# Attention B's score units issued in pairs, with three probability buffers and most other products through PSUM bank 7

## The chip, the cores and the metric

The kernel runs on one core of one Trainium2 chip. The metric is the device time of one execution in microseconds (us). A core has five engines that run side by side: TensorE (PE in the profile; PEld is its weight loads), VectorE (DVE), ScalarE (ACT), GpSimd (POOL) and SyncE (SP, which here issues all DMAs). They are ordered only by semaphores.

## What is computed

A block of four residual layers on x of 16 batches x 512 tokens x 128 channels, all float32:

```python
x = x + attn_a(layernorm(x))   # 16 heads of 64; softmax of q over d, of k over tokens; context = q^T k, then v
x = x + ffn(layernorm(x))      # xr, xk = mix of x and x one token before; sigmoid(xr Wr) * (relu(xk Wk)^2 Wv)
x = x + attn_b(layernorm(x))   # 16 heads of 8, rotary embedding:
#   scores = einsum('bhqd,bhkd->bhqk', q, k) / sqrt(8); attn = softmax(scores); ctx = attn @ v; ctx @ W_O
x = x + ffn(layernorm(x))
```

Attention B has 16 x 16 x 512 x 512 scores, and each goes through an exponential: this and the exponentials of attention A's q and k are ScalarE's main work.

## The kernel before

**Software pipeline.** The program is a row of 20 iterations, i = 0 to 19 (FUSED = NB + 4), written out for each engine by hand. In iteration i the engines work on five batches at once: a = i (attention A: projections, exponentials, context), s = i-1 (the end of attention A and the first feed-forward layer, f1), l = i-2 (layer norm and projections for attention B), b = i-3 (attention B's scores) and e = i-4 (the end of attention B and the second feed-forward layer, f2). Iterations 0 to 2 fill the pipeline (`filling_step`), 4 to 15 have all five stages, 16 to 19 drain it.

**Units.** An iteration has 16 units, n = 0 to 15. In each, TensorE issues `proj_half(n)` (three 512-column products into bank 4: a quarter of a token chunk's q and k), `scores(n)` (four products of 32 rows x 128 columns at four row positions of the array, into banks 0 to 3: four heads, 128 keys, 512 queries), and `weigh_values(n-1)` (four products with 32-column tiles at four column positions, into bank 6: probabilities times values). ScalarE answers with `exp_half(n)` (bank 4, 512 columns) and `exp_scores(n)` (banks 0 to 3, 2,048 columns) into one of two probability buffers. `scores(n)` waits until `exp_scores(n-1)` has emptied the banks, `proj_half(n+1)` until `exp_half(n)` has emptied bank 4.

**The rest** of a batch stands at fixed units between these (the table `places`): `context` (four calls a batch, 16 products each, of 64-column tiles), `ctx_wout`, `wv_ctx_wout`, `attn_out`, `heads_out`, `proj_b` (three parts), four groups of four transposes, and `ffn_k`, `ffn_r`, `ffn_v` for each feed-forward layer. Float32 products run as two passes (eight matmuls for four products). The k and r products and the transposes of h1 go through bank 4, and so lie in line with the projections; the others go through banks 5 and 7. VectorE or ScalarE copies each result out, and the order on each engine is the order in the code.

**Names.** `hold(engine, signal, batch, count)` is a wait. `s_exp`, `s_mm`, `ph_exp`, `ph_mm` count finished score and projection exponentials and products; `pv` counts weighed units; `p_ev` copies of `proj_b`; `h1_sb` the copy of h1's transpose; `t_ev`, `m_ev` the copies of `ctx_wout` and `wv_ctx_wout`.

## Time and profile before

| | |
|---|---|
| median of three runs | 1050.62 us (1045.62, 1050.62, 1050.64) |
| the profiled execution | 1045.19 us, span of its instructions 1043.4 us |
| TensorE matmul busy | 951.9 us (91%) |
| ScalarE busy | 735.1 us (70%) |
| VectorE busy | 610.4 us (58%) |
| GpSimd busy | 507.7 us (49%) |
| granted TensorE clock, mean | 0.971 |
| start of the score products of i = 3, 4, 10, 11, 16, 17 | 105.16, 168.77, 519.55, 577.98, 869.27, 929.15 us |

The starts of successive iterations can be read in the timeline from the first score products of each (four matmuls, L1493, or L1510 where the scores are split). A busy TensorE is not a TensorE at its peak: its matmuls overlap, and the time from one start to the next says more than a duration.

### The profile page before, as it was taken

What the parts mean: (1) busy time and instruction counts of PE and PEld (TensorE: products, weight loads), DVE (VectorE), ACT (ScalarE), POOL (GpSimd) and SP (SyncE); (2) the same over time, 40 slices, a digit from 0 to 9 for tenths busy, and PEclk for the clock granted to TensorE, in tenths of its full rate; (3) what the DMA queues carried; (4) which work ended last, traced back from release to release, by engine and by line L of the source; (5) the groups of instructions that cost most, each with busy time, mean ns of one, the idle gap of its engine ahead of it and who ended that gap; (6) DMA issues with size and microseconds to landing.
All of it is one profiled execution on the core that took longest, in us unless ns stands there. A gap on an engine that the chain in (4) does not pass through costs nothing.

```text
span 1043.4 us, 21070 instructions
## 1 busy us (share of the span) xinstructions
PE 951.9 (91%) x8139; PEld 510.9 (49%) x8139; DVE 610.4 (58%) x1475; ACT 735.1 (70%) x772; POOL 507.7 (49%) x344
## 2 busy tenths in 40 slices
PE   5985889999999999999999999999999999597983
PEld 3874534545454555545454545545554544232322
DVE  5776446566573847556573847656574745655233
ACT  4554667877777777878777777878777776375860
POOL 3758163644727292744637382754637271425000
PEclk9999889999999999999999999999999999798995
DMA  6002222324132332324132232324132232223210
GB/s 174 8 31 90 68 97 69 125 58 133 46 107 87 88 97 83 120 72 127 48 113 78 83 97 82 117 71 132 46 110 69 72 111 72 81 66 101 74 34 15
DMA packets 68657, 87.44 MB, mean 84 GB/s; under 512 B 13633, under 2 KB 40130, under 8 KB 68546
## 3 DMA queue, kind: packets, MB, share of 16 engines
q1 hardware_dynamic: 68546, 85.96, 27.4%
q8 instruction: 69, 1.13, 0.5%
q14 instruction: 42, 0.34, 0.1%
HBM read 16.19 MB, written 20.97 MB: 36 GB/s over the span
## 4 chain that ended last, share of the span: by engine, by line
PE 72%; ACT 14%; DVE 6%; issue 3%; SPq 2%; POOL 2%; DMA 1%; ACTq 0%; DVEq 0%
PE PS L1537 19%; PE PS L1351 8%; ACT work L658 8%; PE PS L1493 7%; PE PS L1407 6%; PE PS L1353 6%; PE PS L1352 5%; PE PS L1346 4%; PE PS L1451 3%; ACT work L652 3%; PE PS L1445 3%; PE PS L1428 3%; PE PS L1458 3%; PE PS L1553 2%; PE PS L1420 2%
## 5 line engine op out<-in xcount | busy, mean ns | idle before, releaser
L658 ACT ACTIVATE work<-PS 128x2048 f32<-128x2048 f32 x224 | 420.8, 1878 | 43.0 <-PE PS L1493 39.0
L1537 PE MATMUL PS<-work,v 128*32 128x512 f32 x2048 | 276.1, 611 | 4.6 <-DVE U L1034 4.1
L652 ACT ACTIVATE work<-PS 128x512 f32<-128x512 f32 x256 | 152.3, 598 | 145.1 <-PE PS L1353 142.9
L426 POOL TENSOR_TENSOR rs<-ve,half_neg 128x4 f32<-128x4 f32 x64 | 65.4, 1022 | 358.7 <-DVE ve L878 358.7
L439 POOL TENSOR_TENSOR work<-work,q_rcp 128x1024 f32<-128x1024 f32 x64 | 121.9, 1904 | 122.0 <-DVE q_rcp L930 122.0
L1493 PE MATMUL PS<-q_st,k_st 32*128 32x512 f32 x896 | 114.5, 501 | 19.6 <-DMA q_st<-qk_lo 10.1
L1351 PE MATMUL PS<-wqk,h1h 128*128 128x512 f32 x256 | 123.7, 483 | 2.6 <-issue 2.6
L1352 PE MATMUL PS<-wqk,h1h 128*128 128x512 f32 x256 | 101.9, 398 | 0.0
L1353 PE MATMUL PS<-wqk,h1l 128*128 128x512 f32 x256 | 101.7, 397 | 0.0
L1493 PEld LDWEIGHTS PS<-q_st,k_st 32*128 32x128 f32 x896 | 43.3, 183 | 108.2 <-issue 76.6
L1351 PEld LDWEIGHTS PS<-wqk,h1h 128*128 128x128 f32 x256 | 48.6, 190 | 86.9 <-ACT work L652 31.0
L927 DVE TENSOR_REDUCE q_sum<-work 128x16 f32<-128x1024 f32 x64 | 77.7, 1214 | 8.4 <-ACT work L652 8.0
L1407 PEld LDWEIGHTS PS<-work 128*64 128x64 f32 x2048 | 65.7, 139 | 33.8 <-ACT work L652 24.9
L1537 PEld LDWEIGHTS PS<-work,v 128*32 128x32 f32 x2048 | 40.5, 108 | 80.1 <-issue 70.7
L1407 PE MATMUL PS<-work 128*64 128x64 f32 x2048 | 74.5, 226 | 0.9 <-POOL work L439 0.9
L979 DVE COPY r_sb<-PS 128x512 f32<-128x512 f32 x30 | 20.7, 691 | 79.4 <-PE PS L1451 79.4
L1051 DVE RECIPROCAL cT<-parted 128x512 f32<-128x512 f32 x13 | 43.6, 3352 | 31.4 <-DMA parted<-U 31.3
L969 DVE TENSOR_SCALAR k_relu<-PS 128x512 f32<-128x512 f32 x32 | 22.0, 688 | 66.4 <-PE PS L1445 66.4
L984 DVE SCALAR_TENSOR_TENSOR gated<-gate,PS 128x512 f32<-128x512 f32 x32 | 21.3, 665 | 66.4 <-PE PS L1458 66.3
L1353 PEld LDWEIGHTS PS<-wqk,h1l 128*128 128x128 f32 x256 | 48.6, 190 | 11.4
L1352 PEld LDWEIGHTS PS<-wqk,h1h 128*128 128x128 f32 x256 | 49.2, 192 | 1.5
L953 DVE SCALAR_TENSOR_TENSOR mixed_k<-PS,mu,mixed_k 128x511 f32<-128x511 f32 x32 | 23.8, 744 | 42.3 <-ACT mixed_k L679 42.1
(159 smaller groups left out, 1611.0 us busy)
## 6 DMA issues: line engine op xcount, KB each, us to landing
qkv_scratch<-qkv_sb SPq DMA_DIRECT2D x16, 768.0 KB, 4.9
rot<-qkv_sb SPq DMA_DIRECT2D x32, 256.0 KB, 3.0
k_st<-qk_hi SPq DMA_DIRECT2D x128, 64.0 KB, 2.1
k_st<-qk_lo SPq DMA_DIRECT2D x128, 64.0 KB, 2.1
q_st<-qk_hi SPq DMA_DIRECT2D x128, 64.0 KB, 2.1
q_st<-qk_lo SPq DMA_DIRECT2D x128, 64.0 KB, 2.1
...
```

The costliest lines, as they stand in the source:

```text
L426: pool.tensor_tensor(rs[:, :], ve[:, :], half_neg[:, :], ALU.pow).then_inc(rstd[n].sem, 1)
L439: pool.tensor_tensor(q3, q3, q_rcp[:, :].unsqueeze(2).to_broadcast([P, HA, DA]), ALU.mult)\
L652: act.activation((EQ, EK)[r // 2][c % 2][:, (r % 2) * 512:(r % 2) * 512 + 512], PS[:, bank, :], ACT.Exp)\
L658: act.activation(probs[n % 2], PS[:, 0:4, :], ACT.Exp).then_inc(z["s_exp"].sem, 1)
L927: dve.reduce_sum(q_sum[:, :], EQ[c % 2].rearrange("p (h d) -> p h d", h=HA), AX_X).then_inc(q_rc.sem, 1)
L1051: dve.reciprocal(cT[:, :], parted[:, 1, :]).then_inc(z["c_rcp"].sem, 1)
L1351: pe.matmul(dst, w[0], h[0], start=True, stop=False)
L1352: pe.matmul(dst, w[0], h[1], start=False, stop=False)
L1353: return pe.matmul(dst, w[1], h[0], start=False, stop=stop)
L1407: mm = pe.matmul(PS[s * DA:s * DA + DA, 5, t * DA:t * DA + DA], EK[c % 2][:, cols], EQ[c % 2][:, cols], start=(c == 0 and t == 0), stop=(c ...
L1493: mm = pe.matmul(PS[:, h, :], k_st[g % 2][rows, kc * P:(kc + 1) * P], q_st[g % 2][rows, :], start=True, stop=True, tile_position=(32 * h, 0))
L1537: mm = pe.matmul(PS[32 * h:32 * h + 32, 6, :], v_flat[p][:, kc, at:at + 32], probs[n % 2][:, h, :], start=(n % 8 == 0), stop=(n % 8 == 7), ...
```

## The change

The lines below are of the core of the diff, with eight columns of indentation taken off. For iterations 3 to 16 every engine gets a `paired_step` of eight pairs, k = 0 to 7, in place of 16 units. On TensorE a pair is: scores of unit 2k; the values of units 2k-2 and 2k-1 (with a `context` ahead of them at k = 4); scores of unit 2k+1; then products that use the whole array: `proj_half(2k)`, one further product, `proj_half(2k+1)`, another one. ScalarE's order becomes scores, half, scores, half. The probability buffers are three. `context` becomes `context_narrow`, which makes the same sums with twice as many products of 32-column tiles. `ffn_k`, `ffn_r` and the transposes of h1 go through bank 7; ScalarE's gate reads its product from PSUM and the copy to `r_sb` is gone. The copies of h1's transpose and of M, two of three `proj_b` copies and both scalings before a `mix` move from ScalarE to VectorE. The transposes of h3 for the next iteration stand at the end of this one.

```diff
-probs = [work[:, 4096 + r * 2048:4096 + (r + 1) * 2048].rearrange("p (j n) -> p j n", j=4) for r in range(2)]
+work_b = sb("work_b", [P, 2048])
+probs = [w.rearrange("p (j n) -> p j n", j=4) for w in (work[:, 4096:6144], work[:, 6144:8192], work_b[:, :])]
...
-qk_rot = sb("qk_rot", [P, 2, N])
-r_sb = sb("r_sb", [P, N])
...
+def iterations(filling_step, paired_step, draining_step):
+    for i in range(FUSED):
+        if i <= 2:
+            filling_step(i, i % 2)
+        elif i <= NB:
+            paired_step(i, i % 2)
+        else:
+            draining_step(i, i % 2)
+def probs_of(z, b, n):
+    return probs[(b + n) % 3] if z is att[0] else probs[n % 2]
...
+    def paired_step(i, p):
+        a, s, l, b, e = i, i - 1, i - 2, i - 3, i - 4
+        z = att[0]
+        stack_k(z, b, 1)
+        stack_q(z, b, 1)
+        if there(e):
+            part_values(z, e, 1)
+        hold(sp, z["roped"], l - 1)
+        hold(sp, p_ev, l, 2)
+        swap_pairs(z, l)
+        stack_k(z, b, 2)
+        stack_q(z, b, 2)
+        if there(a + 2):
+            load_xa(a + 2)
+        store_qkv(l)
+        if there(a):
+            load_xr(a)
+        stack_k(z, b, 3)
+        stack_q(z, b, 3)
+        hold(sp, x2_st, b)
+        load_x2(z, b)
+        if b < LATE:
+            part_values(z, b, 0)
+        store_x2(s)
+        stack_k(z, l, 0)
+        stack_q(z, l, 0)
+        if there(e):
+            store_out(z, ffn[1], e)
...
+    def paired_step(i, p):
+        a, s, l, e = i, i - 1, i - 2, i - 4
+        A, E = there(a), there(e)
+        z, f1, f2 = att[0], ffn[0], ffn[1]
+        if at_batch(i, 3):
+            rsqrt_var(2, l)
+        if there(a + 1):
+            rsqrt_var(0, a + 1)
+        add_bias(s)
+        if A:
+            q_hats(a, 0)
+        if E:
+            hold(pool, p_ev, l, 2)
+            rope_by_cos(z, l)
+            rope_by_sin(z, l)
+            rope_sum(z, l)
+        rsqrt_var(1, s)
+        if A:
+            q_hats(a, 1)
+        if not E:
+            hold(pool, p_ev, l, 2)
+            rope_by_cos(z, l)
+            rope_by_sin(z, l)
+            rope_sum(z, l)
+        if there(a + 1):
+            split_h1(a + 1, 1 - p)
+        if E:
+            rsqrt_var(3, e)
+        hold(pool, f1["v"], s - 1)
+        square(f1, s)
+        if E:
+            ln3_apply(e)
+        if A:
+            q_hats(a, 2)
+        split_qk(z, l)
+        hold(pool, p_ev, l)
+        hold(pool, z["pv"], l - 2)
+        v_copy(z, l, p)
+        rsqrt_var(2, s)
+        if E:
+            hold(pool, f2["v"], e - 1)
+            square(f2, e)
+        if A:
+            q_hats(a, 3)
...
-        hold(act, z["pv"], b, n - 1)
+        if z is att[0]:
+            hold(act, z["pv"], b, n - 2)
+        else:
+            hold(act, z["pv"], b, n - 1)
         hold(act, z["s_mm"], b, n + 1)
-        act.activation(probs[n % 2], PS[:, 0:4, :], ACT.Exp).then_inc(z["s_exp"].sem, 1)
+        act.activation(probs_of(z, b, n), PS[:, 0:4, :], ACT.Exp).then_inc(z["s_exp"].sem, 1)
...
-    def gates_copied(f, j, k):
-        hold(act, f["r_sb"], k)
...
+    def paired_step(i, p):
+        a, s, l, b, e = i, i - 1, i - 2, i - 3, i - 4
+        A, E = there(a), there(e)
+        z, f1, f2 = att[0], ffn[0], ffn[1]
+        for k in range(8):
+            exp_scores(z, b, 2 * k)
+            if E and k == 1:
+                hold(act, qkv_st, l - 1)
+                hold(act, z["swap"], l - 1)
+                hold(act, z["roped"], l - 1)
+                hold(act, z["v_ok"], l - 1)
+                p_copy(l, 1)
+            if k == 2:
+                t_copy(s)
+            if not E and k == 3:
+                hold(act, z["v_ok"], l - 1)
+                p_copy(l, 2)
+            if k == 5:
+                hold(act, f1["x"], s - 1, 1)
+                gates(f1, s, 7)
+            if E and k == 7:
+                hold(act, f2["x"], e - 1, 1)
+                gates(f2, e, 7)
+            if A:
+                exp_half(a, 2 * k, False)
+            exp_scores(z, b, 2 * k + 1)
+            if A:
+                exp_half(a, 2 * k + 1, False)
...
+    def paired_step(i, p):
+        a, s, l, b, e = i, i - 1, i - 2, i - 3, i - 4
+        A, E = there(a), there(e)
+        z, f1, f2 = att[0], ffn[0], ffn[1]
+        if E:
+            split_h3(l)
+            pv_copy(z, e, 1)
+            qkv_free(l)
+            p_copy(l, 0)
+        else:
+            ln_norm(2, l, x2, h3)
+        if there(a + 1):
+            ln1_stats(a + 1)
+        c_norm(s)
+        if not E:
+            split_h3(l)
+        if A:
+            sums_of(a, 0)
+        if there(a + 1):
+            ln1_norm(a + 1)
+        if E:
+            p_copy(l, 2)
+            divide(z, e)
+            look_at(parted[:, 1, :], e, AX_X, 2)
+        else:
+            qkv_free(l)
+            p_copy(l, 0)
+            p_copy(l, 1)
+        m_copy(s)
+        add_x1(s)
+        if A:
+            sums_of(a, 1)
+        ln_norm(1, s, x1, hn1)
+        if there(a + 1):
+            h1_copy(a + 1, 1 - p)
+        if E:
+            add_x3(z, e)
+        scale_and_mix(f1, s)
+        if E:
+            x3_stats(z, 3, e)
+        pv_copy(z, b, 0)
+        hold(dve, f2["act"], e - 1)
+        relu(f1, s, 7)
+        if A:
+            sums_of(a, 2)
+        gate_v(f1, s)
+        if E:
+            scale_and_mix(f2, e)
+        add_x2(s)
+        if E:
+            hold(dve, f1["act"], s)
+            relu(f2, e, 7)
+        if A:
+            sums_of(a, 3)
+        ln_norm(2, s, x2, h3)
+        if E:
+            gate_v(f2, e)
+            hold(dve, z["out_st"], e - 1)
+            add_gated(f2, e, x3, out_sb)
...
+    def context_narrow(a, c):
+        hold(pe, q_hat, a, c + 1)
+        for t in range(PAIRS):
+            for q in range(4):
+                rows = slice(32 * q, 32 * q + 32)
+                head = t * P + q // 2 * DA
+                mm = pe.matmul(PS[rows, 5, t * DA:t * DA + DA], EK[c % 2][:, t * P + 32 * q:t * P + 32 * q + 32],
+                               EQ[c % 2][:, head:head + DA], start=(c == 0 and t == 0), stop=(c == NC - 1),
+                               tile_position=(0, 32 * q), skip_group_check=True)
+        mm.then_inc(c_mm.sem, 1)
...
+    def paired_step(i, p):
+        a, s, l, b, e = i, i - 1, i - 2, i - 3, i - 4
+        A, E = there(a), there(e)
+        z, f1, f2 = att[0], ffn[0], ffn[1]
+        for k in range(8):
+            if at_batch(i, 3) and k == 0:
+                hold(pe, ph_exp, s)
+            scores(z, b, 2 * k)
+            if k == 0 and E:
+                weigh_values(z, e, 14, p)
+                weigh_values(z, e, 15, p)
+            if k == 0 and not E:
+                context_narrow(s, 3)
+            if k == 4 and A:
+                if E:
+                    hold(pe, z["x3_ok"], e)
+                hold(pe, ph_exp, a, 4)
+                context_narrow(a, 0)
+            if k == 1 and not E:
+                hold(pe, f1["x"], s - 1, 1)
+            if k > 0:
+                weigh_values(z, b, 2 * k - 2, 1 - p)
+                weigh_values(z, b, 2 * k - 1, 1 - p)
+            scores(z, b, 2 * k + 1)
+            if A:
+                if at_batch(i, 3) and k == 0:
+                    hold(pe, f1["gate"], s - 1)
+                proj_half(a, p, 2 * k, False)
+            if k == 0 and E:
+                proj_b(l, 0)
+            if k == 1 and E:
+                proj_b(l, 2)
+            if k == 1 and not E:
+                proj_b(l, 0)
+            if k == 2:
+                if not E:
+                    hold(pe, t_ev, s)
+                    proj_b(l, 1)
+                wv_ctx_wout(s)
+            if k == 3:
+                if E:
+                    hold(pe, x1_ok, s)
+                    heads_out(z, e)
+                if there(a + 1):
+                    hold(pe, p_ev, l)
+                    hold(pe, t_ev, s)
+                    head_T(a + 1, 7)
+            if k == 4:
+                hold(pe, f1["mix"], s)
+                ffn_k(f1, s, 7)
+            if k == 5:
+                hold(pe, f1["gate"], s)
+                ffn_v(f1, s)
+            if k == 6 and E:
+                hold(pe, f2["mix"], e)
+                ffn_k(f2, e, 7)
+            if k == 7 and E:
+                hold(pe, f2["gate"], e)
+                ffn_v(f2, e)
+            if A:
+                proj_half(a, p, 2 * k + 1, False)
+            if k == 0 and E:
+                proj_b(l, 1)
+            if k == 0 and not E:
+                hold(pe, p_ev, l - 1)
+                h3_transposes(l)
+            if k == 1:
+                hold(pe, p_ev, l, 3 if E else 1)
+                ctx_wout(s)
+            if k == 2:
+                attn_out(s, 1 - p)
+                if not E:
+                    proj_b(l, 2)
+            if k == 3:
+                if there(a + 1):
+                    hold(pe, h1_sb, a + 1)
+                else:
+                    hold(pe, p_ev, l)
+                ffn_T(f1, 1, s)
+            if k == 4:
+                ffn_r(f1, s, bank=7)
+            if k == 5 and E:
+                hold(pe, f1["x"], s, 1)
+                ffn_T(f2, 3, e)
+            if k == 6 and E:
+                ffn_r(f2, e, bank=7)
+            if k == 7:
+                if E:
+                    hold(pe, f2["x"], e, 1)
+                else:
+                    hold(pe, f1["x"], s, 1)
+                h3_transposes(s)
+            if k == 0 and E:
+                hold(pe, ph_exp, s)
+                context_narrow(s, 3)
+            if k == 5 and A:
+                hold(pe, ph_exp, a, 8)
+                context_narrow(a, 1)
+            if k == 7 and A:
+                hold(pe, ph_exp, a, 12)
+                context_narrow(a, 2)
```

Three places show the move. First TensorE, around the product T W_v (L1428 before, L1478 after) of a full iteration; L1351 to L1353 and L1389 to L1391 are the three products of a `proj_half`, L1493 and L1543 the scores, L1537 and L1587 the values. Before:

```order
L1351 MATMUL PS<-wqk,h1h 128x512
L1352 MATMUL PS<-wqk,h1h 128x512
L1353 MATMUL PS<-wqk,h1l 128x512
L1493 MATMUL PS<-q_st,k_st 128x512 x4
L1537 MATMUL PS<-work,v_1 32x512 x4
L1428 MATMUL PS<-T_sb,WvT 128x128 x8
L1351 MATMUL PS<-h3h,w3h 128x512
L1352 MATMUL PS<-h3l,w3h 128x512
L1353 MATMUL PS<-h3h,w3l 128x512
```

And after, the pair k = 2:

```order
L1543 MATMUL PS<-q_st,k_st 128x512 x4
L1587 MATMUL PS<-work,v_1 32x512 x4
L1587 MATMUL PS<-work_b,v_1 32x512 x4
L1543 MATMUL PS<-q_st,k_st 128x512 x4
L1389 MATMUL PS<-wqk,h1h 128x512
L1390 MATMUL PS<-wqk,h1h 128x512
L1391 MATMUL PS<-wqk,h1l 128x512
L1478 MATMUL PS<-T_sb,WvT 128x128 x8
L1389 MATMUL PS<-wqk,h1h 128x512
L1390 MATMUL PS<-wqk,h1h 128x512
L1391 MATMUL PS<-wqk,h1l 128x512
L1484 MATMUL PS<-M_sb,h1T 128x128 x4
```

The two groups of values now follow each other, and all products on the whole array stand in one row.

Second ScalarE, in a full iteration; L652 and L677 are `exp_half`, L658 and L687 `exp_scores`. Before, around the copy of T:

```order
L652 ACTIVATE work<-PS 128x512
L658 ACTIVATE work<-PS 128x2048
L719 ACTIVATE T_sb<-PS 128x512 x2
L652 ACTIVATE work<-PS 128x512
L658 ACTIVATE work<-PS 128x2048
```

And after:

```order
L687 ACTIVATE work_b<-PS 128x2048
L743 ACTIVATE T_sb<-PS 128x512 x2
L677 ACTIVATE work<-PS 128x512
L687 ACTIVATE work<-PS 128x2048
L677 ACTIVATE work<-PS 128x512
```

The half of unit 2k now stands between the two score exponentials of its pair, behind the copy.

Third VectorE, between the sum x1 (L946 before, L970 after) and the mix of the first feed-forward layer. Before, from the q sums on:

```order
L927 TENSOR_REDUCE q_sum<-work 128x16
L930 RECIPROCAL q_rcp<-q_sum 128x16
L1058 TENSOR_TENSOR x<-PS,x_back 128x512
```

And after:

```order
L951 TENSOR_REDUCE q_sum<-work 128x16
L954 RECIPROCAL q_rcp<-q_sum 128x16
L909 TENSOR_SCALAR hn<-x,mom,rs 128x128 x4
L989 COPY h1T<-PS 128x512
L1089 TENSOR_TENSOR x<-PS,x_back 128x512
L983 TENSOR_SCALAR mixed_k<-PS,mu 128x512
L983 TENSOR_SCALAR mixed_r<-PS,mu 128x512
L977 SCALAR_TENSOR_TENSOR mixed_k<-PS,mu,mixed_k 128x511
L977 SCALAR_TENSOR_TENSOR mixed_r<-PS,mu,mixed_r 128x511
```

The normalisation of x1 and the copy of h1's transpose now stand ahead of x3, and the two scalings, ScalarE's before, are VectorE's.

## Rows read from the trace of the kernel before

**Rows 1.** The page: busy time, and the chain that ended last by engine.

```profile
PE 951.9 (91%) x8139; PEld 510.9 (49%) x8139; DVE 610.4 (58%) x1475; ACT 735.1 (70%) x772; POOL 507.7 (49%) x344
PE 72%; ACT 14%; DVE 6%; issue 3%; SPq 2%; POOL 2%; DMA 1%; ACTq 0%; DVEq 0%
```

**Rows 2.** Stretches of i = 3, 10 and 16: length, busy, clock, DMA share, GB/s.

```profile
105.16:168.77 63.61, 56.83 (x467) 28.86 (x468) 27.64 (x62) 43.29 (x41) 25.80 (x16) 0.91 0.26 78
519.55:577.98 58.43, 57.38 (x506) 30.51 (x505) 36.14 (x90) 45.17 (x45) 31.93 (x22) 1.00 0.31 91
869.27:929.15 59.88, 45.51 (x361) 21.26 (x362) 36.70 (x81) 32.55 (x21) 19.37 (x13) 0.89 0.25 75
```

**Rows 3.** Timeline of one plain unit, PE and ACT: start us, us, what.

```profile
523.77 1.06 PE L1537 MATMUL PS<-work,v 128*32 128x512 f32 x8
523.96 1.88 ACT L658 ACTIVATE work<-PS 128x2048 f32<-128x2048 f32 x1
524.77 0.50 PE L1351 MATMUL PS<-wqk,h1h 128*128 128x512 f32 x1
...
525.78 0.60 ACT L652 ACTIVATE work<-PS 128x512 f32<-128x512 f32 x1
525.89 0.51 PE L1493 MATMUL PS<-q_st,k_st 32*128 32x512 f32 x4
...
526.33 1.07 PE L1537 MATMUL PS<-work,v 128*32 128x512 f32 x8
526.51 1.88 ACT L658 ACTIVATE work<-PS 128x2048 f32<-128x2048 f32 x1
```

**Rows 4.** Timeline of PE: other products, each with the one behind it.

```profile
511.14 1.16 PE L1458 MATMUL PS<-W7T,k_act 128*128 128x128 f32 x8
512.05 0.48 PE L1351 MATMUL PS<-wqk,h1h 128*128 128x512 f32 x1
...
517.57 1.15 PE L1407 MATMUL PS<-work 128*64 128x64 f32 x32
518.65 0.50 PE L1351 MATMUL PS<-wqk,h1h 128*128 128x512 f32 x1
...
527.33 0.38 PE L1415 MATMUL PS<-ident 128*128 128x2 f32 x2
...
528.67 0.50 PE L1351 MATMUL PS<-wqk,h1h 128*128 128x512 f32 x1
...
531.00 2.05 PE L1428 MATMUL PS<-T_sb,WvT 128*128 128x128 f32 x16
532.81 0.48 PE L1351 MATMUL PS<-h3h,w3h 128*128 128x512 f32 x1
...
533.36 0.40 PE L1353 MATMUL PS<-h3h,w3l 128*128 128x512 f32 x1
533.59 0.40 PE L1351 MATMUL PS<-wqk,h1h 128*128 128x512 f32 x1
...
534.06 0.39 PE L1353 MATMUL PS<-wqk,h1l 128*128 128x512 f32 x1
534.38 0.51 PE L1493 MATMUL PS<-q_st,k_st 32*128 32x512 f32 x4
```

**Rows 5.** Timeline of DVE in i = 9 and 10.

```profile
519.58 2.07 DVE L885 TENSOR_SCALAR h<-x,mom,rs 128x128 f32<-128x128 f32 x4
...
538.07 0.68 DVE L946 TENSOR_TENSOR x<-PS,xr 128x512 f32<-128x512 f32 x1
...
540.47 1.22 DVE L927 TENSOR_REDUCE q_sum<-work 128x16 f32<-128x1024 f32 x1
541.72 0.25 DVE L930 RECIPROCAL q_rcp<-q_sum 128x16 f32<-128x16 f32 x1
```

**Rows 6.** Timeline of PE in i = 16: its longest wait.

```profile
907.58 1.11 PE L1346 MATMUL PS<-ident,hn 128*128 128x128 f32 x4 [6.23 <-DVE mixed_r L953]
```

More of the change, by code:

```diff
@@ L1203, in fused @@
-                if B and not draining(i):
-                    pv_copy(z, b, 0)
-                if S:
-                    hold(dve, f2["act"], e - 1)
-                    relu(f1, s)
-                if A and E:
-                    hold(dve, ph_exp, a, 10)
-                    q_sums(a, 2)
-                if S:
-                    hold(dve, f2["gate"], e - 1)
-                    r_copy(f1, s)
-                if E and draining(i):
                     scale_and_mix(f2, e)
-                elif E:
-                    mix(f2, e)
+                add_x2(s)
@@ L1602, in filling_step @@
                         context(a, 0)
-                    if n == at.h1T:
+                    if n == fill.h1T:
                         if S:
```

518 lines of the change are left out of this document (162 added, 356 removed).

## The prediction

> **What bounds the kernel now.** I read the page first: TensorE is busy for 91% of the span and stands for 72% of the chain that ended last [rows 1]. That share hides what its time is spent on, so next came the stretches. The twelve full iterations, i = 4 to 15, take (869.27 - 168.77) / 12 = 58.4 us each; in i = 10 TensorE is busy for 57.38 of 58.43 us at full clock, ScalarE for 45.17 and VectorE for 36.14 [rows 2]. Only the ends look different: i = 3 takes 63.61 us with 56.83 busy, i = 16 takes 59.88 with 45.51 busy, and in both the granted clock is near 0.9 [rows 2]. So there are three places: 12 full iterations that TensorE's own stream sets, and i = 3 and i = 16, which wait.
>
> The timeline of a plain unit gives the step lengths [rows 3]. Values start at 523.77 and the projection at 524.77: 1.00 us. Scores start at 525.89, values 0.44 later. ScalarE's loop: scores at 525.89, their exponential at 526.51 (0.62 later); exponential at 523.96, next scores at 525.89 (1.93 later). Those two make 2.55 us, the shortest unit that ScalarE allows. A projection starting at 524.77 lets its exponential start at 525.78, 1.01 later; that one takes 0.60, and the next ScalarE instruction may start some 0.1 before its end.
>
> The other prices are read as start to start [rows 4]: eight feed-forward matmuls 0.91; `context` 1.08; `ctx_wout` 1.34 (527.33 to 528.67); `wv_ctx_wout` 1.81 for 16 matmuls, so 0.11 each; a stack of three whole-array products 0.78 (532.81 to 533.59). Between two products of one tile shape a start follows 0.23 later (533.36 to 533.59), but 0.32 where scores come next (534.06 to 534.38). So a change of tile shape costs about 0.1 us beyond the work. The Trainium skill (TensorEngine Tiling, Key Properties) says that a change of tiling mode drains the engine; by that rule, the trace agrees.
>
> **The change, by its parts.** Write t for the start of scores(2k), s for the start of scores(2k+1).
>
> *First half of a pair.* Values of two units take at most 2.0 us, so TensorE could reach s at t + 0.44 + 2.0 = 2.44 at the latest; ScalarE allows it at t + 2.55. So s = t + 2.55, and the shape changes saved there are hidden under ScalarE. Only at k = 4, with a context in front, TensorE sets it: s = t + 0.44 + 1.0 + 1.9 = t + 3.4.
>
> *Second half.* scores(2k+1) can't be exponentiated before the half of 2k, since ScalarE takes them in order: projection 0.44 after s, its exponential 1.01 later, 0.5 for it, then 1.93: next t at least s + 3.88. That is a new wait: a pair takes 6.43 us at least. Also proj_half(2k+1) needs bank 4 empty, s + 0.44 + 1.01 + 0.65 = s + 2.10. TensorE's own way is 0.44 + 0.80 (projection) + first product + 0.78 + second product + 0.1 for the shape change. Within the whole-array shape a product is 0.1 cheaper than after a change: 0.81 for eight matmuls, 1.71 for 16, 0.44 for four transposes.
>
> The eight pairs, each 2.55 plus:
> k = 0: 2.10 + 0.78 + 0.78 (`proj_b`) + 0.1 + 1.08 (context) = 4.84, pair 7.39.
> k = 1: 12 matmuls of 0.11 = 1.36; `ctx_wout` waits for VectorE's copy of them: 1.24 + 1.36 + 0.25 + 0.7 = 3.55, + 1.34 = 4.9, pair 7.45.
> k = 2: 1.24 + 1.71 + 0.78 + 0.81 + 0.1 = 4.64, pair 7.2.
> k = 3: bank 7 holds h1's transpose until VectorE has copied it, and VectorE has work ahead of that: x1 and its moments 2.40 (538.07 to 540.47), q sums 1.5 (to 541.72 + 0.25), the normalisation of x1 2.07, the length that L885 has where GpSimd works beside it (519.58), the copy 0.7 [rows 5]. The transposes of x1 can start 6.7 after t; with 0.5 more the pair is 7.2, where 6.45 would do without this wait.
> k = 4: relu on VectorE stands between k and r products in one bank: 3.4 + 1.24 + 0.43 + 1.4 = 6.5, + 0.9 = pair 7.4.
> k = 5 and 7: the transposes wait until the gated product has left bank 7, s + 3.08; + 0.44 + 0.1 + 1.08 = 4.7, pair 7.25 each.
> k = 6: relu again: 3.12 + 0.81 + 0.1 = 4.03, pair 6.6.
> Sum 57.7 against 58.43: **-0.75 us an iteration, -9 us over twelve.** Without the waits for VectorE the pairs would be shorter by 0.2 (k = 1), 0.75 (k = 3), 0.25 (k = 4, 5, 7) and 0.17 (k = 6), 1.9 in all: the work alone shrinks by 2.6, and bank 7 takes back most of it. Bounds: none of these waits, -2.6 an iteration (-31); each of the six 0.6 longer, +2.8 (+34).
>
> *Narrow contexts.* 64 matmuls of 64 columns in place of 32. No row has them. From below they cost what 32 cost now, 1.08, since the columns that move are the same and four positions work at once as for the values; from above, each matmul costs what one of the 32 does, 1.08 / 32 = 34 ns [rows 4], so 64 cost 2.2. I take the low end: four score matmuls occupy 0.51 us together, one of as many columns 0.50 [rows 3], so four positions start within some 10 ns.
>
> *Moved to VectorE.* Two scalings per feed-forward layer (four at about 0.7), two copies, h1 and M: about 4 us more on 36.14 [rows 2], fewer r copies; no bound by sum, only by the places above. ScalarE loses the same and is no bound either: 43 of 57.7. The order on SyncE puts the stacking of q and k for the next batch behind the store of x2; by my walk its last transfer lands 4 us ahead of need. If that cover goes, the next iteration's first scores wait.
>
> *i = 3.* It has no batch e, and two of its `proj_b` parts stand in k = 2 beside the 16 and the eight matmuls. The same rules give 6.4 + 6.9 + 9.5 + 7.2 + 7.2 + 6.7 + 6.4 + 6.4 = 56.7 against 63.61: **-7**, bounds 0 and -9.
>
> *i = 16.* No projections. Now TensorE waits 6.23 us at one place for VectorE's mix, which stands behind both normalisations [rows 6]. In the new order they are apart, and GpSimd does the second. Following the chain x1, moments, normalisation, mix, k, relu, r, gate, v once for each feed-forward layer, with the durations above, gives pairs of 6.6, 6.8, 7.0, 5.4, 7.0, 5.6, 7.0 and 5.6, 51 us against 59.88; i = 17 takes one unit of values more (+0.5): **-8.5**, bounds 0 and -12.
>
> *Tail.* The gate reads PSUM, without a copy of 0.7 in the last chain: **-1**.
>
> Sum: 1045.19 - 9 - 7 - 8.5 - 1 = 1019.7 us, against the profiled execution's own time. The median shown is 5.4 us above that execution and another run 0.4 above it; I add 2 us for runs of that kind and say 1022.
>
> **The rivals.**
> *A. It goes as above,* 1008 to 1033: 0.55. Below 1008, where VectorE is never late: 0.08.
> *B. Bank 7 becomes the bound.* Every product in it waits for a copy, in one order on VectorE. For it: k = 1, 3, 4, 5, 6, 7 all end in such a wait. Against it: VectorE is idle for a third of the time [rows 2]. With 0.3 more at each of these six, 1.8 an iteration: 1022 + 22 = 1044. Chance 0.2 for 1033 and more, a third of it beyond 1045.
> *C. The narrow contexts cost twice: slower.* Four per iteration, 53 in all. At 34 ns a matmul each costs 1.1 more [rows 4]: 1020 + 58 = 1078. It decides from 0.5 us more each (25.5 / 53), 25 ns a matmul. For it: no row here shows a long run of matmuls closer than 34 ns. Against it: the bursts of four. Chance 0.12. The Trainium skill (TensorE: Matmul & The Clock Gate, Part 1) says that start to start never drops below about 25 ns however few the columns. By that figure a context takes 1.6 us, an estimate, and the kernel 1020 + 28 = 1048; the rows of four scores in 0.51 us speak against it for matmuls at different positions.
> *D. The pair's own wait binds everywhere,* because ScalarE's half is late: a pair of 7.6 us and more gives 61 an iteration, 1052 and above. Against it: the floor is 6.43 and six of eight pairs are longer by TensorE's work. Chance 0.05.
> That the order is not changed as said is excluded: it is written out.
>
> **How the numbers follow.** 0.5% of the median, 5 us, is about what can be told from no change: faster is below 1045.4, slower above 1055.9. Faster: 0.55 + 0.08 + 0.13 = 0.76. Same: 0.07 of B and a little of C, 0.08. Slower: 0.16. The range leaves out half of the case below 1008 and what lies above 1046: 1003 to 1046. A's own range is 1008 to 1033.
>
> **What would show it.** Full iterations of 57.7 us, with pairs near 7.4, 7.45, 7.2, 7.2, 7.4, 7.25, 6.6, 7.25, and s at 2.55 after t but at k = 4. L1457, 64 matmuls in about 1.0 us; 1.6 or more is C. Waits of the transposes L1384 for VectorE's h1T at k = 3. i = 3 near 57 and i = 16 near 51 at a higher clock. It would be wrong if a VectorE instruction at bank 7 is late by more than 0.5 us in several pairs, or if the stacks of q and k come late at k = 0.

## The result

The changed kernel takes 1116.19 us, median of 4 runs (1114.96 to 1118.07), against 1050.53 us before: the ratio is 1.0639, interval 1.0603 to 1.0674. It is 6.4% slower, where 1022 us, 3% faster, had been forecast. The profiled execution took 1114.96 us.

The page of the changed kernel: busy time, and the chain that ended last by engine. It answers to [rows 1].

```profile
PE 949.8 (85%) x9835; PEld 541.9 (49%) x9835; DVE 731.6 (66%) x1542; ACT 674.6 (61%) x671; POOL 505.3 (45%) x346
...
PE 52%; DVE 22%; ACT 13%; issue 7%; SPq 2%; POOL 1%; DMA 1%; ACTq 0%; DVEq 0%
```

TensorE's work hardly changed (951.9 to 949.8 us), but its share of the chain fell from 72% to 52% and VectorE's rose from 6% to 22%. VectorE's busy time grew by 121 us, where the forecast moved about 4 us per iteration to it (some 50 us over twelve). Busy time counts an instruction that is held up as busy, and the rest of the growth will turn out to be mostly that.

The stretches of i = 3, 10 and 16 in the changed kernel, against [rows 2]: window, length, busy times of PE, PEld, DVE, ACT, POOL, granted clock, DMA share, GB/s. The three short ones behind them are parts of i = 10.

```profile
106.04:171.81 65.77, 56.82 (x591) 31.85 (x591) 35.78 (x67) 40.01 (x36) 27.86 (x17) 0.87 0.26 79
561.81:626.67 64.86, 57.37 (x640) 32.84 (x634) 46.61 (x96) 40.44 (x37) 31.50 (x21) 0.95 0.27 82
944.97:997.99 53.02, 42.57 (x394) 21.34 (x389) 30.56 (x70) 32.38 (x21) 19.43 (x13) 0.97 0.29 86
571.81:575.20 3.39, 3.39 (x22) 2.57 (x22) 3.36 (x5) 2.40 (x3) 2.65 (x2) 1.00 0.46 174
575.20:579.80 4.60, 0.04 (x2) 0.00 (x1) 4.60 (x4) 0.89 (x2) 4.52 (x3) 0.69 0.38 100
579.80:582.23 2.43, 2.43 (x35) 2.08 (x35) 2.43 (x1) 0.00 (x0) 1.69 (x1) 0.50 0.67 239
```

The spans differ by 1113.2 - 1043.4 = 69.8 us. The twelve iterations i = 4 to 15 take 944.97 - 171.81 = 773.2 us in place of 700.5, +72.7; i = 3 adds 2.2 and i = 16 gives back 6.9. So the loss is in the full iterations. The short stretches show a hole there: 4.6 us in which TensorE does nothing while VectorE and GpSimd are busy throughout, and behind it a stretch at half the clock (0.50, the level of 1.2 GHz).

Start to start of every second score product, read from TensorE's timeline, gives the pairs (us). "i = 15" has no next batch whose h1 must be normalised; E6 is an experiment below.

| pair k | 0 | 1 | 2 | 3 | 4 | 5 | 6 | 7 | sum |
|---|---|---|---|---|---|---|---|---|---|
| forecast | 7.39 | 7.45 | 7.2 | 7.2 | 7.4 | 7.25 | 6.6 | 7.25 | 57.7 |
| changed, i = 10 | 7.45 | 12.97 | 7.64 | 7.91 | 7.45 | 7.31 | 6.81 | 7.32 | 64.86 |
| changed, i = 15 | 7.44 | 7.37 | 7.25 | 7.37 | 7.45 | 7.30 | 6.82 | 7.45 | 58.45 |
| E6, i = 10 | 7.44 | 7.37 | 7.25 | 6.63 | 8.38 | 7.32 | 6.82 | 7.29 | 58.50 |

One pair stands out, k = 1. The timelines of VectorE, GpSimd and TensorE there (start us, us, engine, line, operation, what, idle before it):

```profile
572.21 0.25 DVE L954 RECIPROCAL q_rcp<-q_sum 128x16 f32<-128x16 f32 x1
572.38 6.76 DVE L909 TENSOR_SCALAR h<-xa,mom,rs 128x128 f32<-128x128 f32 x4
579.07 0.68 DVE L997 COPY qkv_sb<-PS 128x512 f32<-128x512 f32 x1
579.67 3.34 DVE L1082 RECIPROCAL cT<-parted 128x512 f32<-128x512 f32 x1
...
572.54 1.91 POOL L458 TENSOR_TENSOR work<-work,q_rcp 128x1024 f32<-128x1024 f32 x1 [1.24 <-DVE q_rcp L954]
574.41 2.35 POOL L471 TENSOR_TENSOR mask_cos<-qkv_sb,cos_t 128x1024 f32<-128x1024 f32 x1
576.72 2.34 POOL L475 TENSOR_TENSOR rot<-rot,sin_t 128x1024 f32<-128x1024 f32 x1
579.14 2.35 POOL L480 TENSOR_TENSOR mask_cos<-mask_cos,rot 128x1024 f32<-128x1024 f32 x1
...
574.21 0.28 PE L1391 MATMUL PS<-w3h,h3l 128*128 128x128 f32 x1
...
579.80 0.59 PE L1465 MATMUL PS<-ident 128*128 128x2 f32 x2 [4.57 <-DVE qkv_sb L997]
580.32 1.98 PE L1470 MATMUL PS<-wout_sb,ctx_hd 64*64 64x128 f32 x32
```

TensorE's `ctx_wout` waits 4.57 us for the copy of `proj_b`'s third part (L997). The copy itself takes 0.68; it is late because the four instructions of `ln1_norm(a + 1)` (L909) stand ahead of it on VectorE and take 6.76 us (0.29, 1.95, 2.39 and 2.38). In the kernel before the four took 1.1 us, with GpSimd idle. Their line in its timeline of VectorE, i = 10:

```profile
535.86 1.11 DVE L885 TENSOR_SCALAR h<-xa,mom,rs 128x128 f32<-128x128 f32 x4 [1.23 <-POOL rs L426]
```

In the changed kernel GpSimd starts q_hats at 572.54, right behind the reciprocal, and two parts of the rotation follow. L909 ends at 579.14, about 0.1 us after GpSimd's instruction that ends at 576.72 + 2.34 = 579.06. The wait costs 4.57, and `ctx_wout` at the low clock takes 2.43 us to the next scores (579.80 to 582.23) where E6 below takes 1.35. That makes 5.65 us; the second half of k = 1 is 5.60 longer than in i = 15.

TensorE's waits for VectorE in i = 10 (us in total, times, longest):

```profile
PE PS L1465 <- DVE qkv_sb L997: 4.6, 1, 4.6
PE PS L1384 <- DVE h1T L989: 1.4, 1, 1.4
```

The second is at k = 3, behind the x1 normalisation, 2.7 us for four.

### The profile page after: what moved, and what is told of

It reads as the page before. It is cut to its first block, busy times and chain, and to the rows that moved or that the text cites. A ratio compares the mean times of both kernels' runs of the same rounds, so it can differ in the third digit from the quotient of the medians.

```text
span 1113.2 us, 24352 instructions
## 1 busy us (share of the span) xinstructions
PE 949.8 (85%) x9835; PEld 541.9 (49%) x9835; DVE 731.6 (66%) x1542; ACT 674.6 (61%) x671; POOL 505.3 (45%) x346
## 4 chain that ended last, share of the span: by engine, by line
PE 52%; DVE 22%; ACT 13%; issue 7%; SPq 2%; POOL 1%; DMA 1%; ACTq 0%; DVEq 0%
PE PS L1543 7%; ACT work L687 7%; PE PS L1587 7%; PE PS L1389 6%; DVE h L909 6%; PE PS L1457 5%; PE PS L1391 4%; PE PS L1390 4%; DVE hn L909 3%; DVE q_sum L951 3%; PE PS L1384 3%; PE PS L1501 3%; ACT work_b L687 3%; PE PS L1508 3%; PE PS L1478 2%
## 5 line engine op out<-in xcount | busy, mean ns | idle before, releaser
L687 ACT ACTIVATE work<-PS 128x2048 f32<-128x2048 f32 x150 | 281.6, 1877 | 134.6 <-PE PS L1543 134.6
L677 ACT ACTIVATE work<-PS 128x512 f32<-128x512 f32 x256 | 152.8, 600 | 163.7 <-PE PS L1391 161.9
L687 ACT ACTIVATE work_b<-PS 128x2048 f32<-128x2048 f32 x74 | 138.9, 1877 | 68.8 <-PE PS L1543 68.8
L1587 PE MATMUL PS<-work,v 128*32 128x512 f32 x1368 | 179.4, 618 | 0.5 <-ACT work L694 0.5
L1543 PE MATMUL PS<-q_st,k_st 32*128 32x512 f32 x896 | 118.1, 516 | 28.1 <-ACT work L687 11.8
L1389 PE MATMUL PS<-wqk,h1h 128*128 128x512 f32 x256 | 125.5, 490 | 5.7 <-issue 2.6
L1543 PEld LDWEIGHTS PS<-q_st,k_st 32*128 32x128 f32 x896 | 44.5, 188 | 143.8 <-ACT work L687 78.7
L1391 PE MATMUL PS<-wqk,h1l 128*128 128x512 f32 x256 | 102.3, 399 | 0.0
L1587 PE MATMUL PS<-work_b,v 128*32 128x512 f32 x680 | 90.7, 606 | 1.3 <-issue 1.3
L909 DVE TENSOR_SCALAR h<-xa,mom,rs 128x128 f32<-128x128 f32 x52 | 79.3, 1596 | 1.3 <-POOL rs L445 1.3
L1389 PEld LDWEIGHTS PS<-wqk,h1h 128*128 128x128 f32 x256 | 48.5, 189 | 59.6 <-issue 29.5
L1587 PEld LDWEIGHTS PS<-work,v 128*32 128x32 f32 x1368 | 35.7, 112 | 73.5 <-issue 71.9
L1457 PE MATMUL PS<-work 128*32 128x64 f32 x3392 | 60.0, 224 | 0.0
L1457 PEld LDWEIGHTS PS<-work 128*32 128x32 f32 x3392 | 51.3, 112 | 13.1 <-issue 13.1
L1391 PEld LDWEIGHTS PS<-wqk,h1l 128*128 128x128 f32 x256 | 48.7, 190 | 11.5
L1465 PE MATMUL PS<-ident 128*128 128x2 f32 x32 | 8.3, 328 | 52.1 <-DVE qkv_sb L997 50.9
L1384 PE MATMUL PS<-ident,hn 128*128 128x128 f32 x128 | 22.2, 299 | 34.1 <-DVE h1T L989 19.4
```

Of the source, the lines that this page charges most:

```text
L677: act.activation((EQ, EK)[r // 2][c % 2][:, (r % 2) * 512:(r % 2) * 512 + 512], PS[:, bank, :], ACT.Exp)\
L687: act.activation(probs_of(z, b, n), PS[:, 0:4, :], ACT.Exp).then_inc(z["s_exp"].sem, 1)
L909: dve.tensor_scalar(dst[:, c, :], src[:, c, :], mom[:, 0, c:c + 1], rs[:, c:c + 1], ALU.subtract, ALU.mult).then_inc(ln[n].sem, 1)
L1389: pe.matmul(dst, w[0], h[0], start=True, stop=False)
L1391: return pe.matmul(dst, w[1], h[0], start=False, stop=stop)
L1457: mm = pe.matmul(PS[rows, 5, t * DA:t * DA + DA], EK[c % 2][:, t * P + 32 * q:t * P + 32 * q + 32], EQ[c % 2][:, head:head + DA], start=(c ...
```

## The experiments

Theory 1: VectorE's normalisation instructions wait for GpSimd's whole instructions, so the copy behind them is late. Theory 2: VectorE's order alone puts the copy too late. Theory 3: narrow contexts and changes of tile shape cost the time. Theory 4: the pairs themselves are too long. "The iteration" is i = 10 where nothing else is said. Times are medians; the ratio is to the kernel before in the same comparison.

### E1 and E2: the order undone, and the rotation taken away

E1, VectorE:

```
                     sums_of(a, 0)
+                if E:
+                    p_copy(l, 2)
                 if there(a + 1):
                     ln1_norm(a + 1)
                 if E:
-                    p_copy(l, 2)
                     divide(z, e)
```

> VectorE's copy of the third part of projection B stands ahead of the normalisation of the next batch's h1 instead of behind it; both instructions are kept, and so is what GpSimd does at that time. Theory 1 (the four normalisation instructions wait for GpSimd's, 6.8 us for four): pair k=1 falls from 12.97 to 7.4 to 7.8 us, the four still take 5 to 7 us, and because the divide and the copy of M stand behind them, pair k=2 grows from 7.64 by about 2.5 us; -2.5 to -3.5 us for each of eleven iterations, 1075 to 1090 us. Theory 2 (only the order on VectorE is wrong, the durations don't matter): nothing is late behind it, iteration 59.3 us, 1050 to 1058 us. Theory 3 (the narrow contexts and the change of tile shape cost the time) and theory 4 (the pairs themselves are too long for ScalarE's exponentials): 1112 to 1118 us, k=1 as before.

1112.7 us, ratio 1.0613 (1.0578 to 1.0648): 3.5 us below the changed kernel, where 26 to 41 were expected, a miss. Timelines of VectorE and TensorE, i = 10:

```profile
567.55 0.69 DVE L997 COPY qkv_sb<-PS 128x512 f32<-128x512 f32 x1 [2.07 <-PE PS L1392]
568.16 6.77 DVE L909 TENSOR_SCALAR h<-xa,mom,rs 128x128 f32<-128x128 f32 x4
574.85 3.34 DVE L1082 RECIPROCAL cT<-parted 128x512 f32<-128x512 f32 x1
578.22 0.69 DVE L1084 TENSOR_TENSOR cT<-parted,cT 128x512 f32<-128x512 f32 x1
...
580.36 2.07 PE L1485 MATMUL PS<-M_sb,h1T 128*128 128x128 f32 x8 [4.28 <-DVE M_sb L993]
```

The copy is on time and pair k = 1 is 7.38 us, but the four still take 6.77 us behind it, again beside the rotation, and now the copy of M behind them is late: TensorE waits 4.28 us at k = 2. Theory 2 falls. I had put the new wait at 2.5 us; it is nearly the whole delay, since VectorE has no slack between these instructions. The total alone would fit theories 3 and 4; that k = 1 fell and k = 2 rose does not.

E2, GpSimd's rotation in the paired steps on 8 of the 512 columns of q and of k (the rest of the rotation is left out):

```
-rope_by_cos(z, l); rope_by_sin(z, l); rope_sum(z, l)
+pool.tensor_tensor(qk_cos[:, :, 0:8], qkv_sb[:, 0:2, 0:8], cos_t[:, :, 0:8], ALU.mult) ... (and so the other two)
```

> GpSimd's three rotary instructions of the paired steps work on 8 of 512 columns in each half (the rest of the rotation is left out, so the queries and keys of attention B are not rotated); VectorE's order is kept. Theory 1 (VectorE's normalisation waits for GpSimd): the instruction that stood beside q_hats still waits 1.9 us, the two beside the rotation take 0.3 us each, four in 2.7 to 3.2 us in place of 6.8; pair k=1 8.3 to 9.3 us, iteration 60.3 to 61.5, 1062 to 1080 us. Theory 2 (order on VectorE alone): the copy is behind the same instructions, so k=1 stays within 0.5 us of 12.97 and the time above 1105 us. Theories 3 and 4 (narrow contexts, pair structure): 1112 to 1118 us.

1057.4 us, ratio 1.0085 (1.0052 to 1.0119). VectorE's order is the changed kernel's; from the timelines of both engines:

```profile
535.08 2.66 DVE L916 TENSOR_SCALAR h<-xa,mom,rs 128x128 f32<-128x128 f32 x4
...
535.24 1.91 POOL L458 TENSOR_TENSOR work<-work,q_rcp 128x1024 f32<-128x1024 f32 x1 [1.25 <-DVE q_rcp L961]
537.10 0.22 POOL L583 TENSOR_TENSOR mask_cos<-qkv_sb,cos_t 128x16 f32<-128x16 f32 x1
```

Without the long rotation the same four take 2.66 us, of which one waits for q_hats, and k = 1 is 7.79. 59 of the 66 us are gone with no change on VectorE, some 5 us more than the best that I had expected: the expectation kept the 1.08 us that `ctx_wout` loses at the low clock, and the clock no longer falls here (granted clock 0.973 over the run, 0.942 in the changed kernel).

### E3 and E4: the normalisation on ScalarE, and wide contexts

E3:

```
 VectorE:  -ln1_norm(a + 1)   +ln_shift(0, a + 1)
 ScalarE:  +act.activation(h1[:, c, :], xa[:, c, :], ACT.Identity, bias=shifts[0][:, c:c + 1],
 +                          scale=stats[0][3][:, c:c + 1])    (one behind each of the halves 2 to 5)
```

> In the paired steps the normalisation of the next batch's h1 goes from four VectorE instructions to four ScalarE instructions, one after each of the half exponentials 2 to 5; VectorE keeps one small instruction for the shift. GpSimd is as before. Theory 1: k=1 falls to 7.4 to 7.8 us, ScalarE's extra 0.35 to 0.4 us per half are inside its idle time or add at most 0.4 us in k=1 and k=2; iteration 58.4 to 59.8 us, 1043 to 1058 us, thus the time of before or a little less. Theory 2 gives the same. Theories 3 and 4: over 1105 us, and theory 4 above 1120, since ScalarE has 1.5 us more per iteration to do between the exponentials.

1051.5 us, ratio 1.0028 (1.0008 to 1.0047). ScalarE's four take 0.49 us each in the middle of the same GpSimd work, and the iteration is 58.86 us, k = 1 7.37, so theory 4 falls: the extra work between the exponentials costs nothing. Rows of ScalarE, grouped over i = 10 (busy us, mean ns):

```profile
L724 ACT ACTIVATE h<-xa,shift,rs 128x128 f32<-128x128 f32 x4 | 2.0, 490 | 0.0
```

E4, `context_narrow` replaced by `context` in the paired steps:

> The contexts of the paired steps go back from 16 groups of four 32-row products to the pairs of 64-row products of before; all else stays. Theories 1, 2 and 4: a context that lay 1.1 us on TensorE takes 0.8 to 1.3 us and the switch of tile shape before it comes back; the iteration moves by less than 0.8 us, 1108 to 1124 us, k=1 still above 12.5 us. Theory 3 (the narrow contexts are the cost): 1050 to 1080 us.

1125.2 us, ratio 1.0724 (1.069 to 1.0758), 9 us slower than the changed kernel. For the contexts theory 3 falls with the sign reversed: the narrow form helps. Timelines of one context with the scores behind it, narrow in the changed kernel:

```profile
568.23 1.10 PE L1457 MATMUL PS<-work 128*32 128x64 f32 x64
569.26 0.51 PE L1543 MATMUL PS<-q_st,k_st 32*128 32x512 f32 x4
```

and wide in E4:

```profile
572.75 1.15 PE L1445 MATMUL PS<-work 128*64 128x64 f32 x32
573.83 0.50 PE L1543 MATMUL PS<-q_st,k_st 32*128 32x512 f32 x4
```

Start to start it is 1.03 us for 64 narrow products and 1.08 for 32 wide ones. The sum is just outside the range that I gave. In i = 10 the wide form costs 0.25 us (65.11 against 64.86), in the mean of i = 4 to 14 0.66. Half of the 0.66 is in the first half of k = 2, behind the hole, which takes 4.30 us in i = 7 and 11 against 3.00 and 2.94 in the changed kernel; only the rest lies at the contexts.

### E5 to E7: the same work where GpSimd is idle

E5 moves `ln1_norm(a + 1)` ahead of `sums_of(a, 0)`, so ahead of the q_rcp for which q_hats waits. E6 also moves `ln_norm(1, s, x1, hn1)` and `h1_copy` ahead of `sums_of(a, 1)`:

```
                 c_norm(s)
+                if there(a + 1):
+                    ln1_norm(a + 1)
                 if A:
                     sums_of(a, 0)
-                if there(a + 1):
-                    ln1_norm(a + 1)
 ...
                 add_x1(s)
-                if A:
-                    sums_of(a, 1)
                 ln_norm(1, s, x1, hn1)
                 if there(a + 1):
                     h1_copy(a + 1, 1 - p)
+                if A:
+                    sums_of(a, 1)
```

> Only VectorE's order in the paired steps: the four normalisation instructions of the next batch's h1 stand ahead of the q sums instead of behind them, so that they run while GpSimd has no long instruction; the third part's copy is still behind all of them, engines and work are those of the changed kernel. Theory 1 (the instructions wait for GpSimd's): they take 1.1 to 2.0 us for four, the copy ends about 574.3 in the changed kernel's time instead of 579.7, k=1 is 7.4 to 8.3 us and the iteration 58.7 to 59.8, 1046 to 1060 us. A theory in which these instructions are long for another reason (operands, a clock of VectorE) has them at 6.8 us for four wherever they stand and k=1 at 12.5 to 13 us, 1110 to 1118 us.

E5: 1051.1 us, ratio 1.0017 (1.0 to 1.0034), iteration 58.84, k = 1 7.36.

> As the run with the h1 normalisation first, and also the normalisation of x1 (and the copy of h1T behind it) ahead of the second q sums. Theory 1: the x1 normalisation falls from 2.7 us to 1.1, the transposes at k=3 wait 0 to 0.3 us instead of 1.4, iteration 57.4 to 58.2 us; in i=3, where the same instruction waits for the rotation, k=3 falls from 11.2 us to 7 to 8 and the iteration from 65.5 to 60 to 61.5; 1030 to 1043 us. If the wait at k=3 has another cause: as the run before it, within 3 us.

E6: 1042.1 us, ratio 0.991 (0.9874 to 0.9946), 0.9% faster than the kernel before. Timelines of VectorE and GpSimd:

```profile
527.01 1.19 DVE L909 TENSOR_SCALAR h<-xa,mom,rs 128x128 f32<-128x128 f32 x4
528.12 1.21 DVE L951 TENSOR_REDUCE q_sum<-work 128x16 f32<-128x1024 f32 x1
529.36 0.25 DVE L954 RECIPROCAL q_rcp<-q_sum 128x16 f32<-128x16 f32 x1
530.57 0.69 DVE L997 COPY qkv_sb<-PS 128x512 f32<-128x512 f32 x1 [0.96 <-PE PS L1391]
...
543.79 1.11 DVE L909 TENSOR_SCALAR hn<-x,mom,rs 128x128 f32<-128x128 f32 x4 [1.21 <-POOL rs L445]
...
529.70 1.90 POOL L458 TENSOR_TENSOR work<-work,q_rcp 128x1024 f32<-128x1024 f32 x1 [2.34 <-DVE q_rcp L954]
```

and from TensorE's waits of the same iteration (us in total, times, longest):

```profile
PE PS L1457 <- DVE x L1089: 0.9, 1, 0.9
```

Same engines, same instructions, two places moved on VectorE: 6.76 us become 1.19, and the copy waits for TensorE instead of the reverse. This is theory 1. The wait at k = 3 (1.4 us for h1T in the changed kernel) is gone too, pair 7.91 to 6.63; 0.9 of it comes back at k = 4, where TensorE waits for add_x3 behind the sums. i = 3 falls from 65.8 to 61.4.

E6's gain over the kernel before does not lie in the full iterations. In the two profiled executions i = 4 to 15 take 701.7 us in E6 and 700.5 before; i = 3 gains 2.2 and i = 16 5.3, and what lies behind i = 16 loses 2.9.

> The h1 normalisation on ScalarE as in the third run, and the x1 normalisation ahead of the second q sums on VectorE. Theory 1: as the run with both normalisations first, plus or minus 3 us, since ScalarE's 1.9 us per iteration were hidden: 1030 to 1044 us. If ScalarE's work is close to the path once the waits are gone (theory 4), this one is slower than that run by 4 us or more.

E7 (E3 with the second of the two moves): 1042.0 us, ratio 0.9921 (0.9898 to 0.9944), iteration 58.52. ScalarE's extra work costs nothing here either, against theory 4.

### E8: what the third buffer is worth

E6 with `probs[n % 2]` for both attentions and an exponential that waits for the values of unit n - 2.

> As the run with both normalisations first, but attention B has two probability buffers again, so that a unit's exponential waits until the values of the unit two before are done. It prices the third buffer. If the pairs are set by TensorE's own work (busy 55.9 of 59 us in the runs so far), the price is 0 to 0.5 us per pair at most: 1030 to 1075 us, I take 1050. If the third buffer did nothing in this structure: within 3 us of the run with both first.

1144.4 us, ratio 1.0906 (1.0875 to 1.0936), 102 us above E6; I had put it at 0 to 0.5 us a pair. Every first half is 3.50 us in place of 2.55. Waits of TensorE and of ScalarE in i = 10:

```profile
PE PS L1540 <- ACT work L684: 9.1, 8, 1.1
...
ACT work L684 <- PE PS L1584: 15.9, 8, 3.2
```

With two buffers exp(2k) can't start until values 2k - 2 are done, which in a pair stand behind scores(2k): one values group of 0.9 us on ScalarE's loop, eight times. That is the 2.55 of the forecast plus 0.95, and it shows the first half to be ScalarE's. The iteration is 66.39 us, 7.9 more than E6's.

### E9 and E12: chasing the rest

E9 is E6 with `add_x3` also ahead of `sums_of(a, 1)`.

> As the run with both normalisations first, and add_x3 too stands ahead of the second q sums on VectorE. In that run TensorE waited 0.9 us at k=4 for VectorE's add_x3, behind the sums. Theory 1 (each of these waits is VectorE's order around its waits for GpSimd, and TensorE's own work is what is left): first half of k=4 falls from 4.12 to 3.2 us, iteration 57.4 to 57.8 us, 1028 to 1036 us. If the pair is held by something else at k=4 (the value copies, a transfer): 1040 to 1044 us.

1045.2 us, ratio 0.996 (0.9943 to 0.9977), not better than E6, a miss. The first half of k = 4 falls from 4.12 to 3.19 us as expected, but the second grows from 4.26 to 5.64: the sums now stand ahead of the mix and the relu. Waits of TensorE in i = 10:

```profile
PE PS L1501 <- DVE k_relu L1001: 1.5, 1, 1.5
```

E12 also moves the second sums behind the relu, and the second q_hats behind the normalisation of x3 on GpSimd.

> As the run with add_x3 first, and the second q sums go behind the relu on VectorE, with the second q_hats behind the square and the normalisation of x3 on GpSimd. In the run before, TensorE waited 1.5 us at k=4 for VectorE's relu, behind the sums. Theory 1 (what is lost is always the next instruction of VectorE's full stretch at k=3 and k=4, and TensorE's own work is what is left): second half of k=4 falls from 5.64 us to 4.2 to 4.5, iteration 57.4 to 57.9 us, 1026 to 1036 us. If the sums' delay costs a wait at k=5 or k=6 (the context of chunk 1 waits for q_hats): 58 to 59.5 us, 1037 to 1050 us. Whichever it is, the floor of the pair structure with three buffers, eight pairs of 6.8 to 7.45 us, is above 57 us against 58.4 in the kernel before.

1044.7 us, ratio 0.9954 (0.994 to 0.9968): not the total of theory 1 but that of the second case. The iteration is 58.32, second half of k = 4 4.26; but k = 6 now waits 0.83 us for the other layer's relu, and in i = 3 nothing stands between the x1 normalisation and the rotation any more. Timelines of VectorE and GpSimd there:

```profile
135.36 7.31 DVE L908 TENSOR_SCALAR hn<-x,mom,rs 128x128 f32<-128x128 f32 x4 [1.21 <-POOL rs L445]
...
135.23 2.37 POOL L471 TENSOR_TENSOR mask_cos<-qkv_sb,cos_t 128x1024 f32<-128x1024 f32 x1
137.55 2.36 POOL L475 TENSOR_TENSOR rot<-rot,sin_t 128x1024 f32<-128x1024 f32 x1
139.99 2.34 POOL L480 TENSOR_TENSOR mask_cos<-mask_cos,rot 128x1024 f32<-128x1024 f32 x1
```

i = 3 is 65.9 us again, against 61.4 in E6: it is the same wait, met at another place by a move on GpSimd. Shortest of each pair over E6, E9 and E12: 7.43, 7.37, 7.25, 6.63, 7.45, 7.31, 6.82, 7.30, sum 57.6. No full iteration with a next batch had all of them at once.

### E10: how VectorE waits

The changed kernel, with each rotary instruction as two of half the length:

```
-pool.tensor_tensor(qk_cos, qkv_sb[:, 0:2, :], cos_t, ALU.mult)
+pool.tensor_tensor(qk_cos[:, 0, :], qkv_sb[:, 0, :], cos_t[:, 0, :], ALU.mult)
+pool.tensor_tensor(qk_cos[:, 1, :], qkv_sb[:, 1, :], cos_t[:, 1, :], ALU.mult)    (and so the other two)
```

> The changed kernel, with each of GpSimd's three rotary instructions cut into two of half its length (the same elements, the same order). It asks how VectorE waits. If a GpSimd instruction holds VectorE's off for its whole length and VectorE gets one in at each boundary: the four normalisation instructions end after q_hats and two halves, 0.3 + 1.9 + 1.2 + 1.2 = 4.6 us in place of 6.8, k=1 10.6 to 11.2 us in place of 12.97, 1090 to 1098 us. If the two engines share a port's bandwidth evenly, or the instruction is long for another reason: 6.3 to 7 us, 1112 to 1120 us.

1099.0 us, ratio 1.0466 (1.044 to 1.0493). Timelines:

```profile
561.13 4.61 DVE L918 TENSOR_SCALAR h<-xa,mom,rs 128x128 f32<-128x128 f32 x4
...
569.63 1.60 DVE L1093 TENSOR_TENSOR cT<-parted,cT 128x512 f32<-128x512 f32 x1
...
561.30 1.90 POOL L458 TENSOR_TENSOR work<-work,q_rcp 128x1024 f32<-128x1024 f32 x1 [1.25 <-DVE q_rcp L963]
563.16 1.28 POOL L582 TENSOR_TENSOR mask_cos<-qkv_sb,cos_t 128x512 f32<-128x512 f32 x1
564.40 1.26 POOL L583 TENSOR_TENSOR mask_cos<-qkv_sb,cos_t 128x512 f32<-128x512 f32 x1
```

The four take 4.61 us, the 4.6 of the expectation, and k = 1 is 10.82 (the total is 1 us above the range): one VectorE instruction gets in at each end of a GpSimd instruction, here of 1.3 us as before of 2.35. Sharing of bandwidth would have left 6.8, since GpSimd moves the same elements. The Trainium skill (SBUF — State Buffer, "Who interferes with whom") says that VectorE and GpSimd share a port pair under an exclusive lock held for a whole instruction, that `tensor_scalar` and `copy` can take it and that `tensor_reduce` never contends. The trace agrees for `tensor_scalar`, with 1.94, 1.32 and 1.30 us for the last three of the four here, and for `tensor_reduce`: q_sum took 1.21 to 1.22 us beside GpSimd's xr + b_all and with GpSimd idle. For `copy` these iterations show nothing, since their copies read PSUM.

### E11: narrow contexts in the kernel before

> The kernel before with only the narrow contexts (32 columns of keys to a product instead of 64, twice the products). By the run with wide contexts in the changed kernel, 0.7 us per iteration for the narrow ones in pairs: here, where a unit's interval is set by ScalarE as often as by TensorE, 0 to 0.5 us per iteration, 1043 to 1052 us. If the narrow contexts cost time by the number of their products: 1055 to 1075 us.

1045.4 us, ratio 0.9959 (0.9942 to 0.9977): a small gain of 0.4% from this part alone, at the low end of the cost that the forecast chose.

## Why the prediction was wrong

**The step that failed** is the term of k = 1: "`ctx_wout` waits for VectorE's copy of them: 1.24 + 1.36 + 0.25 + 0.7 = 3.55". The 0.25 leaves VectorE free when the products end. It isn't: the products end at 574.21 + 0.28 = 574.5, and the copy starts at 579.07, 4.6 later, with L909 ahead of it. Two things were missing. The prediction names nothing that is queued on VectorE ahead of this copy, and so gives the h1 normalisation no price; its 0.25 would have held with the 1.1 us of the kernel before (572.38 + 1.1 = 573.5, before the products end), but GpSimd's q_hats and rotation now run at that time. At k = 3 I did use the contended length, 2.07 us for the same line in [rows 5]; the measured one is 2.66. Even that row would have given too little at k = 1, since the price is a whole GpSimd instruction for each of VectorE's: 0.3 + 1.9 + 2.4 + 2.4. E2, E5 and E10 showed it each from a different side.

**"No bound by sum, only by the places above"** was right by sum (VectorE 46.61 of 64.86 us busy, 10.5 more than before, of which some 5.7 are this waiting), but the list of places had no queue in it.

**The pairs.** In the changed kernel's i = 10 five of eight lie within 0.21 us of the forecast; beside k = 1, k = 2 is 0.44 longer (the clock behind the hole) and k = 3 0.71 (a normalisation that is contended for longer). With the wait taken away (E6) the sum is 58.50, and 57.6 if each pair had its best, for a forecast of 57.7. s = t + 2.55 held but for k = 2 behind the hole (2.94), and t + 3.4 at k = 4 is 3.2. So most pairs were sized rightly, but no run shows the gain that their sum promised: -0.75 us an iteration was forecast, E6 has +0.07 (58.50 against 58.43) and E12, the best, -0.11 (58.32). In i = 15, which has no h1 to normalise, the changed kernel takes 58.45 us and E9 57.60, but the kernel before only 57.27. The term of -9 us for twelve iterations would thus have failed without the hole too.

**Narrow contexts** were sized rightly at the low end, 1.03 us against 1.08. Rival C, twice the cost, is refuted by E4 and E11. The Trainium skill's floor of about 25 ns from start to start (TensorE: Matmul & The Clock Gate, Part 1) doesn't hold here: 1.03 us / 64 is 16 ns for products at four positions, so the measurement decides.

**Rival B**, bank 7 as the bound by 0.3 us at six places, described the kind of failure but not its size or place: one copy late by 4.6 us. **Rival D** is refuted by i = 15 (58.45) and by E5. Its price was also mis-added: eight pairs of 7.6 us are 3.1 more than 57.7, and twelve times that on 1022 is 1059, not 1052.

**i = 3**: 65.8 in place of 56.7. Waits there:

```profile
PE PS L1384 <- DVE h1T L989: 4.5, 1, 4.5
```

It is the same mechanism at k = 3, where the rotation runs beside the x1 normalisation; E6 takes it away (61.4). Of the 4.7 us that remain in E6, 1.9 are in k = 0, where the granted clock is 0.50 behind the 10.8 us for which TensorE waits for the first q, 1.3 in k = 5, where it waits as long for GpSimd's k_act, and 2.0 in k = 7, of which 1.3 are in the first half, at a clock that has fallen again (0.80 over the pair); the other pairs are 0.5 shorter than forecast in sum.

**i = 16**: 53.0 in place of 51, and i = 17 took 1.8 longer than before where 0.5 was forecast, so the two gain 5.1 of the 8.5. The forecast had the waits for relu right at k = 4 (7.04 for 7.0), but k = 6 took 8.09: its r products, behind a wait of 2.0 us like that of k = 4, took 2.05 us in place of 1.13. The clock is the difference, 0.58 over the stretch that holds them (989.50 to 992.06) and 1.00 at k = 4. In TensorE's waits of i = 16 and in its timeline:

```profile
PE PS L1501 <- DVE k_relu L1001: 3.8, 2, 2.0
...
977.27 1.13 PE L1501 MATMUL PS<-W7T,mixed_r 128*128 128x128 f32 x8 [1.84 <-DVE k_relu L1001]
990.09 2.05 PE L1501 MATMUL PS<-W7T,mixed_r 128*128 128x128 f32 x8 [1.98 <-DVE k_relu L1001]
```

**The tail** did not gain: what lies behind i = 16 took 114.2 us before and 115.2 now, and the start was 0.9 later.
